# State-space stage of a perceiver block: B's rows reach the 128 partitions through DRAM instead of through TensorE

## The reference, cut to what matters

```
proj = xc @ xproj_w
dtp = proj[..., :DTR]
Bm = proj[..., DTR:DTR + DS]
Cm = proj[..., DTR + DS:]
delta = jax.nn.softplus(dtp @ dt_w + dt_b)
A = -jnp.exp(A_log)
dA = jnp.exp(delta[..., None] * A)
dBu = (delta * xc)[..., None] * Bm[:, :, None, :]
...
h = dA_t * h + dBu_t
return (h, jnp.einsum('bds,bs->bd', h, C_t))
```

## Time and profile before

| what | value |
|---|---|
| median of 3 runs | 1899.9 us (1899.02 to 1900.85) |
| the profiled execution's own time | 1897.5 us |
| its span | 1895.8 us |
| PE busy | 1640.8 us (87%) |
| DVE busy | 1204.7 us (64%) |
| ACT busy | 731.3 us (39%) |
| POOL busy | 457.0 us (24%) |

### The profile page before, as it was taken

One profiled execution on the slowest core, in us unless ns is written; L12 is line 12 of the kernel. 1 busy time (PEld: TensorE's weight loads), 2 busy tenths in 40 slices (PEclk: granted clock), 3 DMA queues, 4 the chain that ended last, 5 costly groups with the idle time before them and its releaser, 6 DMA issues. The chain is left out here.

```text
span 1895.8 us, 30570 instructions
## 1 busy us (share of the span) xinstructions
PE 1640.8 (87%) x12408; PEld 1259.5 (66%) x12408; DVE 1204.7 (64%) x1414; ACT 731.3 (39%) x975; POOL 457.0 (24%) x274
## 2 busy tenths in 40 slices
PE   5999989999989999999999999377457775999999
PEld 4777767777767777767777776154234333788888
DVE  4686586576586576586576585545459994644444
ACT  3444354334344334354443343112274330434332
POOL 4200041000041000031000000110049991445552
PEclk9999999999999999999999999587569998899999
DMA  4000120000120000120000000200000001111100
GB/s 153 12 18 1 45 73 1 12 18 1 35 84 1 13 9 10 33 77 10 12 10 9 1 1 1 58 1 0 15 0 1 0 1 42 59 56 44 55 11 23
DMA packets 43356, 47.88 MB, mean 25 GB/s; under 512 B 5200, under 2 KB 30672, under 8 KB 43232
## 3 DMA queue, kind: packets, MB, share of 16 engines
q1 hardware_dynamic: 43232, 46.07, 7.9%
HBM read 45.02 MB, written 1.05 MB: 24 GB/s over the span
## 5 line engine op out<-in xcount | busy, mean ns | idle before, releaser
L493 DVE TENSOR_REDUCE xa_maxes<-psum 128x2 f32<-128x1024 f32 (+1 forms) x288 | 332.5, 1161 | 267.1 <-PE psum L674 267.1
L419 ACT ACTIVATE xa_probs<-psum 128x1024 f32<-128x1024 f32 x272 | 268.9, 1026 | 323.7 <-PE psum L707 310.8
L514 DVE TENSOR_TENSOR xa_prob_sum<-xa_prob_sum,xa_probs 128x1024 f32<-128x1024 f32 x240 | 308.8, 1287 | 11.2 <-ACT xa_probs L419 10.4
L719 PE MATMUL psum<-xa_probs,xa_vals 128*64 128x256 f32 x2176 | 263.1, 385 | 2.2 <-DVE xa_heads_T L528 1.6
L719 PEld LDWEIGHTS psum<-xa_probs,xa_vals 128*64 128x64 f32 x2176 | 146.5, 136 | 92.8 <-issue 23.8
L344 POOL TENSOR_TENSOR xa_w_lo<-xa_stage,xa_w_hi 128x768 fp32r<-128x768 f32 x16 | 31.9, 1994 | 617.2 <-ACT xa_w_hi L379 617.2
L606 PE MATMUL psum<-xa_wv_hi,xa_ctx_hi 128*128 128x256 f32 x512 | 149.0, 291 | 21.3 <-DVE xa_maxes L493 18.5
L701 PE MATMUL psum<-xa_q_hi,xa_k_hi 64*128 64x256 f32 x1088 | 156.3, 283 | 0.6 <-issue 0.6
L705 PE MATMUL psum<-xa_q_hi,xa_k_lo 64*128 64x256 f32 x1088 | 154.4, 280 | 0.0
L707 PE MATMUL psum<-xa_neg_max,xa_ones 64*128 64x256 f32 x1088 | 154.1, 279 | 0.0
L703 PE MATMUL psum<-xa_q_lo,xa_k_hi 64*128 64x256 f32 x1088 | 153.9, 279 | 0.0
(11 more groups left out here) (275 smaller groups left out, 3434.6 us busy)
## 6 DMA issues: line engine op xcount, KB each, us to landing
xa_ctx_in<-in_ctxT_dram SPq DMA_DIRECT2D x32, 512.0 KB, 3.7
xa_stage<-in_L_xattn_Wk_dram SPq DMA_DIRECT2D x32, 128.0 KB, 2.3
xa_stage<-in_L_xattn_Wv_dram SPq DMA_DIRECT2D x16, 256.0 KB, 2.9
ex_raw<-in_L_ffn_w_gate_dram SPq DMA_DIRECT2D x8, 512.0 KB, 3.6
ex_raw<-in_L_ffn_w_up_dram SPq DMA_DIRECT2D x8, 512.0 KB, 4.4
ex_raw<-in_L_ffn_w_down_dram SPq DMA_DIRECT2D x8, 512.0 KB, 3.7
xa_stage<-in_L_xattn_Wq_dram SPq DMA_DIRECT2D x16, 128.0 KB, 2.3
X<-in_x_dram SPq DMA_DIRECT2D x1, 1024.0 KB, 5.6
```

The costliest lines, as they stand in the source:

```text
L419: nc.scalar.activation(probs[:, n % RING, :], S[:, 2 * (n % 2):2 * (n % 2) + 2, :].rearrange("p h q -> p (h q)"), ACT.Exp, scale=HD ** -0. ...
L493: dve.tensor_reduce(maxes[:, qt, :, g:g + 1], max_banks(v, g, qt)[:, :, 0:group_keys(g)[1]], AX_X, ALU.max).then_inc(max_reduced, 1)
L514: dve.tensor_tensor(prob_sum[:, :], prob_sum[:, :], probs[:, n % RING, :], ALU.add).then_inc(summed, 1)
L719: i = pe.matmul(O[half[h], 0:N1], vals[:, 2 * j + t, lanes:lanes + HD], probs[:, n % RING, (2 * h + t) * N1:(2 * h + t + 1) * N1], start=( ...
```

## The change

The 16 rows of B are written once from `proj` to a DRAM tensor, and read back spread over the 128 partitions in four transfers, of 1, 3, 4 and 8 rows. SP issues all five, the store after `proj_stored`, the reads after the store has landed. Each read has a semaphore of its own, and POOL waits for it in `make_drive`. PE's 32 matmuls that spread B, and the 32 copies of ACT and DVE, are gone. The clearing of the decay buffers waits for `dt_biased` (the bias additions of delta, the last readers of those banks) in place of the copies. The rows of C are spread as before.

```diff
+        GROUPS = ((0, 1), (1, 4), (4, 8), (8, 16))
+        scratch = nc.dram_tensor("ss_scratch", (DS, NT), F32, kind="Internal").ap()
+        scratch_stored = sem("scratch_stored")
+        b_loaded = [sem(f"b_loaded{i}") for i in range(len(GROUPS))]
@@ sync @@
+            sp.wait_ge(proj_stored, 2)
+            sp.dma_start(scratch, proj[DTR:DTR + DS, :]).then_inc(scratch_stored, 16)
+            sp.wait_ge(scratch_stored, 16)
+            for i, (lo, hi) in enumerate(GROUPS):
+                sp.dma_start(b_rows[:, lo:hi, :].rearrange("p s n -> p (s n)"),
+                             scratch[lo:hi, :].rearrange("(a s) n -> a (s n)", a=1).broadcast_to([P, (hi - lo) * NT])
+                             ).then_inc(b_loaded[i], 16)
@@ gpsimd, make_drive @@
-                    pool.wait_ge((b_stored_a, b_stored_v)[s % 2], s // 2 + 1)
+                    pool.wait_ge(b_loaded[[lo <= s < hi for lo, hi in GROUPS].index(True)], 16)
@@ scalar @@
-            for r in range(0, DS, 2):
-                for h in range(2):
-                    act.wait_ge(spread, 2 * r + h + 1)
-                    i = nc.scalar.activation(b_rows[:, r, h * HT:(h + 1) * HT], banks[2 * (r % 4) + h][:, 0:HT],
-                                             ACT.Copy)
-                i.then_inc(b_stored_a, 1)
@@ vector @@
-            for r in range(1, DS, 2):
-                for h in range(2):
-                    dve.wait_ge(spread, 2 * r + h + 1)
-                    i = dve.tensor_copy(b_rows[:, r, h * HT:(h + 1) * HT], banks[2 * (r % 4) + h][:, 0:HT])
-                i.then_inc(b_stored_v, 1)
-
-            dve.wait_ge(b_stored_a, DS // 2)
-            dve.wait_ge(b_stored_v, DS // 2)
+            dve.wait_ge(dt_biased, 2 * CT)
@@ tensor @@
-            for r in range(DS):
-                if r >= 4:
-                    pe.wait_ge((b_stored_a, b_stored_v)[r % 2], (r - 4) // 2 + 1)
-                spread_row(r, banks[2 * (r % 4):2 * (r % 4) + 2]).then_inc(spread, 2)
-            pe.wait_ge(b_stored_a, DS // 2)
-            pe.wait_ge(b_stored_v, DS // 2)
```

More of the change, by code:

```diff
@@ L1361, in state_space @@
         a_ready = sem("a_ready")
-        spread = sem("spread")
-        b_stored_a = sem("b_stored_a")
-        b_stored_v = sem("b_stored_v")
+        GROUPS = ((0, 1), (1, 4), (4, 8), (8, 16))
+        scratch = nc.dram_tensor("ss_scratch", (DS, NT), F32, kind="Internal").ap()
+        scratch_stored = sem("scratch_stored")
+        b_loaded = [sem(f"b_loaded{i}") for i in range(len(GROUPS))]
         c_spread = sem("c_spread")
```

## The result

The changed kernel has a median of 1889.8 us (ten runs, 1888.0 to 1894.3), the kernel before 1898.4 on the same chips (ten runs, 1893.4 to 1900.9). The ratio is **0.9963, with a 95% interval of 0.9951 to 0.9975: 7.0 us less**, or 0.37%. It is taken from the means, 1890.6 against 1897.6 us; the medians lie 8.6 us apart. The profiled execution took 1888.15 us, with a span of 1886.4.

A forecast was written before the change was run, and what follows sets the result against it. DVE sets the loop's pace, so only its first scan's start matters: 7.1 us earlier, plus 0.1 for PE's clock, gives -7.0 us. The median goes from 1899.9 to 1892.9 us, range 1890.7 to 1896.9.

The forecast's parts named there:

- The bank thread: Ahead of the scan loop: B's spreads and copies, then clearing, table load, first decay; removing them starts the loop 7.1 us earlier.
- The loop follows as a whole: State-space scan loop: drives stay ready and POOL's wait for C shrinks, so the whole 7.1 us comes through.
- the stated range: The forecast's range for the kernel's median time, 1890.7 to 1896.9 us.
- Store and reads: SP's transfers of B: store landed by 1373.4, last group by 1397.2 at 295 GB/s, all in time and hidden.
- 165 / 0.56: Read rate of B: 165 GB/s for spread vector rows, engines busy 0.56 of the time, giving 295 GB/s when busy.
- the bound above, from plain rows: Upper bound on the read rate of B, 384 GB/s, at which plain rows went.
- Rivals A and B: Reads of B: A, last group late at POOL's drive 8, 1898.2 us, a tenth; B, slower than before, 1909.8 us, 0.07.
- 155 GB/s: The rate at which the reads of B, 6.29 MB, must stream to hide everything.
- The figure of 103 GB/s: Skill's rate for 128-partition streams in lock-step; reads of B would take 61 us, kernel slower by some 13 us.
- Rival C: Scan loop: starts early, but PE at its low clock holds it back; 1897 to 1898 us, chance 0.04.
- POOL's and DVE's slack would forgive a little: In the loop, late reads of B: a caveat to the 132 GB/s needed to lose nothing against before; no size given.

The follow-up runs named there:

- E1: Changed kernel with the 32 spreading matmuls and 32 copies put back into an unread tile, decay buffers cleared after them; ratio to the kernel before 1.0001.
- E2: Changed kernel with SP holding the store until all eight bias additions of delta are done; ratio to the kernel before 0.9972.
- E11: Changed kernel whose last read takes 128 different 24 KB rows of other data instead of one row 128 times; profiled execution 1890.5 us.
- E3: Changed kernel with SP holding the store until DVE's last softplus; ratio to the kernel before 0.9985.
- E5: Changed kernel with 58 extra matmuls keeping PE busy until just before the loop's first steps; ratio to the kernel before 0.9963.
- E10: E9 with first drives ahead of later dx, two dx inside the loop, decay buffers cleared before the softplus; ratio to the kernel before 0.9917.
- E7: Changed kernel with ACT's work regrouped, Abs and Exp of all tiles, then the four Ln; ratio to the kernel before 0.9947.
- E9: E7 with ACT writing its Ln to PSUM, so DVE's softplus has one input there; ratio to the kernel before 0.9930.
- E4: Changed kernel with 28 extra matmuls on PE in its idle stretch ahead of the loop; ratio to the kernel before 0.9980.

## Why the prediction was right, point by point

- **The bank thread is what the change removes: right, and shown** (E1). First scan predicted 7.1 us earlier, measured 7.10. Shifted by 3.34 us, the clearing stands at 1395.94 (predicted 1396.05), the first decay ends at 1398.27 (1398.3) and the first scan starts at 1399.80 (1399.8); POOL's drive is what it waits for, as named.
- **The loop follows as a whole: right.** The wait for the first row of C is 0.96 us, predicted 0.9, and up to the 57th scan the loop keeps the old pace to within 0.2 us. The last product ends at 1562.6 when shifted; "about 1561" was predicted (1568.1, the old end, less 7.1), and the 1.6 us between are the longer loop. The forecast was -7.0 us and the means differ by 7.0; that they agree so closely is luck. In the two profiled executions this block is only 3.9 us shorter (7.1 less 1.6 and 1.6), and the rest of the 9.4 lies in blocks with the same code. Loop and tail vary by 2.2 and 1.6 us among kernels with the same code there, and ten executions of the changed kernel spread over 6.2 us. As a time, the median of 1889.8 us lies 0.9 below the stated range; part of this is that the kernel before had a lower median too, 1898.4 in ten executions against 1899.9 in the three that the forecast started from.
- **Store and reads: hidden, as predicted; all sizes on the pessimistic side.** The store landed after 1.7 us (taken: 2.9), and the reads ran at 422 GB/s (taken: 295; upper bound 384). The last group landed 20.9 us behind the copy of `proj`; the prediction gives 27.6. The step that mis-sized it was "165 / 0.56": a window of loads of 1 KB per partition says little of runs of 9 to 24 KB (that the length of the run is what differs was not tested by itself). Even the bound above, from plain rows, was too low. Neither touched the time, since the reads are hidden (E2: 19 us later, still free).
- **Rivals A and B: refuted.** There was no wait of POOL on a transfer, and the rate stayed far above 155 GB/s. The figure of 103 GB/s, by which the prediction weighed the Trainium skill against the trace (DMA: Bandwidth & Descriptors, "Latency and other measured facts"), is for a large pitch between partitions; E11 shows that a pitch of zero acts as distinct rows do. That A's mechanism exists once the margin is gone is shown by E3.
- **Rival C: its condition came, its price did not.** PE was low at the loop's start (2.76 us a sum), but it was so before the change too, and the 17th scan stands 38.28 us behind the first, against 38.26: 0.02 us, where I took 0.1. Taking the low clock away (E5) brings 0.7 us up to that step and nothing in the whole loop. DVE's waits for PE rose from 2.5 to 4.2 us, of which 1.5 is the one wait near the loop's end; in the first ten steps they are 0.7 us together, far below the 3 that would have spoken for C.
- **"POOL's and DVE's slack would forgive a little": not decided.** In E3 4.41 us of lateness at the first scan cost 4.2 us by the ratios against the changed kernel, 2.5 against E2.

## What to carry to other kernels

Replacing a chain of engine work by transfers gains what the chain added to the path at its end, not the work that it did (here 7 us from 32 copies and 32 matmuls), and no more than its lead over the next thread: POOL's first drive, ready 7.2 us ahead of its scan before the change, now sets the first scan. Going after that one as well (E10) more than doubled the gain. Where the data exist long before they are needed, ask only when a transfer must be issued to be in time, and test the margin by holding it back. When work is newly put side by side on DVE and POOL, do not add up durations measured alone.

## What the runs showed of the hardware

- DVE and POOL hold each other up when both run operations of two tensors that all lie in SBUF: a softplus that starts while POOL is at a `dx` takes 2.56 us instead of 0.96, a `dx` beside a softplus about 2.5 instead of 1.80 (E7). With one of DVE's inputs in PSUM neither slows (E9: 0.95 and 1.81 each). The Trainium skill, SBUF — State Buffer, "Who interferes with whom", says that a DVE instruction with two SBUF inputs contends with a POOL instruction that reads SBUF, and that the ports they share are an exclusive lock. The traces agree on both: in E7 the one that started later ended about its own duration behind the other's end (1389.1 and 1388.3 for the fourth softplus).
- Runs of 9 to 24 KB, read from DRAM by each of 128 partitions, streamed at 422 GB/s; with distinct 24 KB runs in the last group it was 424 (E11). A 48 KB store to DRAM landed in 1.7 us.
- In E4 PE's clock rose from 1.2 to 2.4 GHz while the 28 extra matmuls ran, and was at 1.2 GHz again when the loop's first steps came, 5.7 us after the last of them.
- The same code's stages differ between executions and kernels by short stretches at the lower clock: 28.40 us of tail at 1.00, 30.04 at a mean of 0.94.
